# Second attention of a small vision model: queries and keys laid out as four channels of a whole image per partition

## The chip, the cores and the metric

One core of a Trainium2 chip runs the whole program. The metric is device time in microseconds (us) from one launch, the median of several runs.

## What is computed

The model has two layers on 8 images of 16x16 pixels with 192 channels. Each layer adds an attention and then a mixture of experts to its input. The change touches the attention of the second layer only:

```python
def _dilate_attention(q, k, v, head_dim, scale, ksz, dil):
    qr = q.reshape(B, nh, head_dim, L)
    kp = _unfold(k, ksz, dil).reshape(B, nh, head_dim, kk, L)
    vp = _unfold(v, ksz, dil).reshape(B, nh, head_dim, kk, L)
    attn = jnp.einsum('bncl,bnckl->bnlk', qr, kp) * scale
    attn = jax.nn.softmax(attn, axis=-1)
    out = jnp.einsum('bnlk,bnckl->bnlc', attn, vp)
...
for g in range(G):
    qkv = jnp.einsum('oi,bihw->bohw', qkv_w, xg[g])
    qkv = qkv.reshape(nd, 3, B, gd // 3, H, W)
    for i in range(nd):
        outs.append(_dilate_attention(qkv[i, 0], qkv[i, 1], qkv[i, 2], hd, scale, KSZ, DILATIONS[i]))
```

Here a pixel attends to its 3x3 neighbours (kk = 9) at a distance of 1, 2 or 3 pixels (the dilation), zero outside the image. There are 4 groups and 8 images, so 32 group-images for each dilation, and a head of 16 channels.

## The kernel before

The program runs in stages, one after the other on five engines: the first attention, the first mixture of experts (MoE), the second attention (about 455 to 612 us of the profiled span), the second MoE. Each engine executes its own list of instructions in the order in which the code below issues them, and waits on semaphores.

In the second attention the dilations are worked through in the order 3, 2, 1 (index i = 2, 1, 0 in the code; `position(i)` is 0, 1, 2). TensorE makes queries, keys and values (L1865), ScalarE copies them from PSUM to `stage` (L1956), and they are stored to the DRAM tensor `qkvd` in three phases of four DMAs (`store_qkv`: phase 0 on SyncE's queue, phases 1 and 2 on GpSimd's). Then they are loaded back in another layout (`load_qkv`, L1688): the first queries by GpSimd, all the rest by SyncE, in the order keys of dilation 3; queries, keys of dilation 2, values of dilation 3; queries, keys of dilation 1, values of dilations 2 and 1. SyncE waits for the stores of a phase before the loads that need them.

The layout before: a partition holds one group-image and one quarter of the rows (4 quarters x 32 group-images = 128 partitions), with all 16 channels of 4 rows of 16 pixels. Keys (`k1`, in the tile `kk`) and values (`v1`, in `qq`) carry a halo of d rows above and below, whose rows outside the image ScalarE fills with zeros during the first MoE (`clear_edges`, L1696). Queries (`q1`) lie in `pk` and `xn`. VectorE clears the border columns of the products once, before it combines the first MoE's results (`clear_columns`).

The work per dilation, with three groups of three neighbours (a group `col` has one horizontal shift; the first, here called the middle column, has none):

- `products` (VectorE, L1761): nine multiplications of queries by shifted keys into `prod`, one buffer for all dilations, so a group waits until TensorE has read the same group of the dilation before.
- `channel_sums` (TensorE, L1877): for each group 16 matmuls, one per channel, with the 128x128 identity as weights, 3 x 64 columns each, summed in PSUM. A matmul in float32 is two records in the profile.
- `scores` (VectorE), `exponentials` (ScalarE), `weights` (VectorE): the softmax over nine neighbours; ScalarE's `copy_scores` brings the sums from PSUM first.
- `values` (VectorE, L1789): nine products of weights and shifted values into six `term` buffers. For dilation 3 all nine terms go to TensorE; for dilations 2 and 1 VectorE adds two of each three itself (L1819), and TensorE gets six.
- `neighbour_sums` (TensorE, L1895): two matmuls with the identity for each term, one per half of the channels.
- `value_sums` (ScalarE, L1974): the copy of the sum from PSUM, then SyncE stores it to `y1d`.

The order on each engine is written out by hand. VectorE: products(2), products(1), scores(2), products(0, 0), weights(2), values(2), products(0, 1), products(0, 2), scores(1), weights(1), values(1), scores(0), weights(0), values(0). TensorE: channel_sums(2), channel_sums(1), neighbour_sums(2), channel_sums(0), neighbour_sums(1), neighbour_sums(0), then 12 filler matmuls (L1930) while the result goes through DRAM. ScalarE:

```python
copy_scores(2)
exponentials(2)
copy_scores(1)
value_sums(2)
exponentials(1)
copy_scores(0)
exponentials(0)
value_sums(1)
value_sums(0)
```

## Time and profile before

| | us |
|---|---|
| median of 3 runs (lowest to highest) | 837.42 (832.13 to 838.84) |
| the profiled execution | 838.17 |
| its span, first to last instruction | 836.4 |
| TensorE busy in the span | 750.3 (90%) |
| VectorE busy | 412.8 (49%) |
| ScalarE busy | 305.1 (36%) |
| GpSimd busy | 384.2 (46%) |

Times in the trace are us from the start of the span. PE is TensorE (matmuls), PEld its weight loads, DVE VectorE, ACT ScalarE, POOL GpSimd, SP SyncE. L1761 is line 1761 of the kernel. Each row of a group of instructions ends with the time for which the engine had stood idle before them, and with what ended that. TensorE overlaps its matmuls, so the mean duration of one is longer than the time by which it moves the work on; that time is the length of a run of matmuls divided by their number.

### The profile page before, as it was taken

Reading aid. Unit: us, or ns where it says so; the run is one execution under the profiler, and the core shown is the slowest. Engines: PE = TensorE matmul, PEld = TensorE weight load, DVE = VectorE, ACT = ScalarE, POOL = GpSimd, SP = SyncE. Lnnn points to the kernel's source line nnn. Section 1 sums busy time; section 2 is a strip of 40 time slices with the busy share of each in tenths; the row PEclk is TensorE's granted clock in tenths of the full one; section 3 lists DMA queues with packets and bytes.
Section 4 is the critical chain, followed back from the end, with each engine's and each line's share of the span. In section 5 each row is a group of like instructions: output and inputs, shape, how many; then the busy total and the mean of one; then the engine's idle time right before and its main releaser. Section 6 shows DMA issues by size and latency. Waiting matters only on the chain.

```text
span 836.4 us, 19543 instructions
## 1 busy us (share of the span) xinstructions
PE 750.3 (90%) x6156; PEld 642.6 (77%) x6157; DVE 412.8 (49%) x999; ACT 305.1 (36%) x862; POOL 384.2 (46%) x789
## 2 busy tenths in 40 slices
PE   7989999999988999999980689998987999999980
PEld 4768878888745999999980459783655999999980
DVE  4354564567566333433316336998276333433315
ACT  2434464455651423424340640011260433424330
POOL 8754453420134677777731030000044677777730
PEclk9797999999998999999995699999998999999995
DMA  7595663663683111111104199400794111111106
GB/s 239 165 213 139 154 147 105 168 133 75 218 302 128 42 48 53 40 55 55 49 18 150 37 263 196 72 26 25 272 337 138 46 49 53 45 55 51 44 17 226
DMA packets 61082, 97.21 MB, mean 116 GB/s; under 512 B 25711, under 2 KB 43844, under 8 KB 61032
## 3 DMA queue, kind: packets, MB, share of 16 engines
q1 hardware_dynamic: 43560, 62.28, 27.2%
q0 software_dynamic: 17472, 34.27, 13.8%
q8 instruction: 31, 0.51, 0.3%
q14 instruction: 19, 0.16, 0.1%
HBM read 66.23 MB, written 31.52 MB: 117 GB/s over the span
## 4 chain that ended last, share of the span: by engine, by line
PE 58%; DVE 13%; issue 10%; POOL 9%; DMA 5%; ACT 2%; SPq 1%; POOLq 1%; DVEq 0%; ACTq 0%
PE ps L1498 11%; PE ps L1482 9%; PE ps L1490 5%; PE ps L779 4%; PE ps L1877 4%; DVE x_sb L1425 3%; PE ps L809 2%; POOL credit L1554 2%; POOL yd L1572 2%; PE ps L1895 2%; DVE arena L1789 2%; PE ps L829 2%; PE ps L755 2%; POOL xnT L1562 2%; PE ps L853 2%
## 5 line engine op out<-in xcount | busy, mean ns | idle before, releaser
L1536 ACT ACTIVATE arena<-ps,b1s 128x128 f32<-128x128 f32 x468 | 123.9, 410 | 241.4 <-PE ps L1490 241.3
L1498 PE MATMUL ps<-arena 128*128 x936 | 158.7, 329 | 1.2 <-ACT arena L1536 1.2
L1498 PEld LDWEIGHTS ps<-arena 128*128 128x128 f32 x936 | 151.4, 190 | 3.7 <-issue 1.6
L1482 PE MATMUL ps<-xnT 128*128 128x128 f32 x936 | 112.2, 280 | 1.9 <-DVE xnT L1376 1.9
L1482 PEld LDWEIGHTS ps<-xnT 128*128 128x128 f32 x936 | 111.0, 197 | 2.3 <-DVE xnT L1376 2.3
L275 POOL TENSOR_TENSOR rstd<-veps,cst 128x4 f32<-128x4 f32 (+1 forms) x12 | 14.9, 1238 | 191.0 <-DVE veps L269 191.0
L1554 POOL TENSOR_TENSOR credit<-credit 1x1 f32<-1x1 f32 x306 | 70.4, 230 | 48.1 <-DVE xnT L1382 19.0
L1562 POOL DMA_INDIRECT xnT<-xnd,gcur x78 | 79.1, 1014 | 17.4 <-issue 12.4
L626 DVE TENSOR_REDUCE rt<-ps 98x2 f32<-98x392 f32 x96 | 53.0, 563 | 65.8 <-PE ps L809 65.8
L1388 DVE COPY xnT<-arena 128x768 f32 x78 | 43.9, 563 | 69.2 <-PE ps L1482 65.9
L1572 POOL DMA_INDIRECT yd<-rt,scur x52 | 57.7, 1110 | 27.0 <-issue 20.6
L1068 ACT ACTIVATE arena<-ps 98x392 f32<-98x392 f32 x96 | 46.7, 499 | 63.6 <-PE ps L829 63.2
L1490 PE MATMUL ps<-xnT,rt 64*128 64x128 f32 x936 | 59.2, 278 | 0.0
L1382 DVE TENSOR_TENSOR rt<-ps,xn 128x192 f32<-128x192 f32 x52 | 18.6, 358 | 80.5 <-PE ps L1498 80.5
L1490 PEld LDWEIGHTS ps<-xnT,rt 64*128 64x128 f32 x936 | 54.3, 188 | 3.1
L1877 PE MATMUL ps<-arena,cst 128*128 128x192 f32 x288 | 48.9, 334 | 3.3 <-DVE arena L1761 3.3
L1877 PEld LDWEIGHTS ps<-arena,cst 128*128 128x128 f32 x288 | 48.5, 195 | 4.0 <-DVE arena L1761 3.7
L809 PE MATMUL ps<-kk,qq 114*98 114x196 f32 x192 | 43.0, 309 | 1.9 <-DMA kk<-kd 1.6
L779 PEld LDWEIGHTS ps<-xnT,arena 128*112 128x112 f32 (+2 forms) x448 | 37.0, 173 | 7.7 <-issue 3.9
L779 PE MATMUL ps<-xnT,arena 128*112 128x32 f32 (+4 forms) x448 | 39.6, 261 | 3.6 <-POOL xnT L571 3.6
L1394 DVE COPY rt<-arena 128x384 f32 x78 | 28.3, 363 | 28.1 <-PE ps L1490 25.0
L1895 PE MATMUL ps<-arena,cst 128*128 128x512 f32 (+3 forms) x84 | 34.1, 558 | 3.1 <-DVE arena L1819 3.1
(216 smaller groups left out, 1243.5 us busy)
## 6 DMA issues: line engine op xcount, KB each, us to landing
arena<-in_w SPq DMA_DIRECT2D x16, 576.0 KB, 10.3
arena<-in_w1a SPq DMA_DIRECT2D x16, 384.0 KB, 6.7
arena<-yd SPq DMA_DIRECT2D x8, 768.0 KB, 7.1
kk<-kd SPq DMA_DIRECT2D x48, 96.0 KB
qq<-qd SPq DMA_DIRECT2D x16, 264.0 KB
qq<-qd SPq DMA_DIRECT2D x16, 192.0 KB
arena<-in_w1b SPq DMA_DIRECT2D x16, 192.0 KB, 7.0
qkvd<-arena POOLq DMA_DIRECT2D x8, 384.0 KB, 8.2
```

The source lines that it names most:

```text
L626: m = nc.vector.tensor_reduce(mxa[0:WAH, cc, 2 * u:2 * u + 2, j], ps[0:WAH, SM + u, 0:2 * WA].rearrange("p (q n) -> p q n", q=2), AX.X, AL ...
L779: last = mm(o, relt[w][0:rows, at, 0:cols], q, start=True, stop=True)
L809: last = mm(ps[0:WAH, SM + u, c * WA:(c + 1) * WA], q[:, at:at + WAH], k[:, u * WA:(u + 1) * WA], start=True, stop=True)
L1482: last = mm(hidden(r, f), wcura[r][:, f * P:(f + 1) * P], xgT[r][:, 0, :], start=f < 2, stop=False, skip_group_check=True)
L1490: last = mm(hidden(r, f), wcurb[r][rows, f // 2 * P:(f // 2 + 1) * P], xgT[r][rows, 1, :], start=False, stop=f >= FT - 2, skip_group_check ...
L1498: last = mm(product(r), hidT[r][:, f, :], w2s[:, e, f, :], start=f == 0, stop=f == FT - 1)
L1536: last = nc.scalar.activation(hidT[r][:, f, :], hidden(r, f), ACT.Gelu, bias=b1s[l][:, bass.ds(e * FT + f, 1)])
L1554: nc.gpsimd.tensor_tensor(credit[0:1, 12 + kind:13 + kind], credit[0:1, 0:1], credit[0:1, 0:1], ALU.add)\
L1562: nc.gpsimd.indirect_dma_start(out=xg[r], out_offset=None, in_=xnd[l], in_offset=bass.IndirectOffsetOnAxis(ap=gcur[:, r:r + 1], axis=0))\
L1572: nc.gpsimd.indirect_dma_start(out=yd[l], out_offset=bass.IndirectOffsetOnAxis(ap=scur[:, r:r + 1], axis=0), in_=ys[r], in_offset=None, bo ...
L1877: last = mm(to.rearrange("p (n x) -> p n x", n=3), ident, prod[:, 3 * col:3 * col + 3, c, :], start=c == 0, stop=c == HD - 1)
L1895: last = mm(dst, ident, src, start=k == 0, stop=k == len(terms) - 1, skip_group_check=True)
```

## The change

Queries and keys get another layout: a partition now holds one group-image and a quarter of the channels (4 channels, `CHQ`), for the whole image of 256 pixels. No halo is needed for them, since all rows are in the partition. Each load of queries or keys is four DMAs of 32 partitions x 4 channels x 256 pixels, so runs of 1 KB. Products are formed over the part of the image for which the neighbour exists, so rows outside the image are skipped, too; `clear_columns` clears the border rows of `prod` besides its border columns, and the zeros in the key halos (six of ScalarE's twelve instructions) go. The channel sum now runs over 4 channels in a partition and over 4 groups of partitions: for each channel and each quarter of the pixels, one matmul with a 128x32 weight matrix `fold` (four identities of 32 on top of one another, appended to the constants) sums the four partition groups and writes the 32 partitions of that pixel quarter, so that the scores come out in the layout that the softmax and the values had before. There are still 16 matmuls per group of neighbours. Values keep their layout. VectorE's additions of value products go: TensorE sums nine terms for every dilation.

```diff
@@ -146,7 +146,7 @@
         at = 0
         CST, CST_AT = {}, {}
         for name, n in (("ident", 128), ("rev", E), ("lt", E * E), ("tok", TILES), ("iots", SLOTS), ("ones", 1), ("power", 1),
-                        ("tri", P // 2), ("iot", P // 2), ("mask", 2 * TILES * E + E), ("slots", SLOTS // 2)):
+                        ("tri", P // 2), ("iot", P // 2), ("mask", 2 * TILES * E + E), ("slots", SLOTS // 2), ("fold", 32)):
             CST[name], CST_AT[name] = cst[:, at:at + n], at
             at += n
         ident = CST["ident"]
@@ -1631,23 +1631,24 @@
 
             return max(0, -dx * d), SIDE - d * abs(dx)
 
-        k1, v1, k_edges = [], [], []
+        CHQ = HD // 4
+        k1 = [kk[:, i * CHQ * PIX:(i + 1) * CHQ * PIX].rearrange("p (c y x) -> p c y x", c=CHQ, x=SIDE).bitcast(F32)
+              for i in range(len(DIL))]
+        v1, edges = [], []
         at1 = 0
         for d in DIL:
             n = HD * halo(d) * SIDE
-            for views, home in ((k1, kk), (v1, qq)):
-                rows_ = home[:, at1:at1 + n].rearrange("p (c y x) -> p c y x", c=HD, x=SIDE)
-                views.append(rows_.bitcast(F32))
-                k_edges += [rows_[0:32, :, 0:d, :], rows_[96:P, :, QR + d:QR + 2 * d, :]]
+            rows_ = qq[:, at1:at1 + n].rearrange("p (c y x) -> p c y x", c=HD, x=SIDE)
+            v1.append(rows_.bitcast(F32))
+            edges += [rows_[0:32, :, 0:d, :], rows_[96:P, :, QR + d:QR + 2 * d, :]]
             at1 += n
         q_home = [pk[:, :, :].rearrange("p h n -> p (h n)").bitcast(F32)[:, k * HD * QPIX:(k + 1) * HD * QPIX] for k in range(2)]
         q_home.append(xn[:, :, :, :].rearrange("p u t c -> p (u t c)")[:, 0:HD * QPIX])
-        q1 = [home.rearrange("p (c y x) -> p c y x", c=HD, x=SIDE) for home in q_home]
+        q1 = [home.rearrange("p (c y x) -> p c y x", c=CHQ, x=SIDE) for home in q_home]
 
         stage = ar(0, [QKV_UNITS, GRP * PIX], KC)
-        prod = ar(QKV_UNITS * GRP * PIX, [NN, HD, QPIX])
+        prod = ar(QKV_UNITS * GRP * PIX, [NN, CHQ, PIX])
         term = [ar(k * HD * QPIX, [HD, QPIX]) for k in range(TERMS)]
-        second_term = ar(TERMS * HD * QPIX, [HD, QPIX])
         acc = [ar((TERMS + 1 + i) * HD * QPIX, [QPIX * HD]) for i in range(3)]
         yl = xt_(0, [TILES, C])
         sc = [rt[:, i * NN * QPIX:(i + 1) * NN * QPIX] for i in range(3)]
@@ -1678,9 +1679,13 @@
 
             d = DIL[i]
             dst = (q1, k1, v1)[t]
-            src = qkvd[:, (i * 3 + t) * SPU:(i * 3 + t + 1) * SPU].rearrange("c b g x -> (b g) c x")
-            edge = d if t else 0
-            for quarter in range(4):
+            units = slice((i * 3 + t) * SPU, (i * 3 + t + 1) * SPU)
+            src = qkvd[:, units].rearrange("c b g x -> (b g) c x")
+            for quarter in range(4 if t < 2 else 0):
+                eng.dma_start(dst[i][quarter * 32:(quarter + 1) * 32].rearrange("p c y x -> p c (y x)"),
+                              src[:, quarter * CHQ:(quarter + 1) * CHQ]).then_inc(s_(f"{'qkv'[t]}_in{i}"), 16)
+            edge = d
+            for quarter in range(4 if t == 2 else 0):
                 lo = max(0, quarter * QR - edge)
                 hi = min(SIDE, (quarter + 1) * QR + edge)
                 row = lo - (quarter * QR - edge)
@@ -1691,7 +1696,7 @@
         def clear_edges(act):
 
             zero = CST["lt"][:, 0:1]
-            for edge in k_edges:
+            for edge in edges:
                 parts = edge.shape[0]
                 nc.scalar.activation(edge, zero[0:parts].unsqueeze(2).unsqueeze(3).broadcast_to(list(edge.shape)), ACT.Copy)\
                     .then_inc(s_("edges_clear"), 1)
@@ -1700,13 +1705,17 @@
 
             rows_ = prod.rearrange("p n c (y x) -> p n (c y) x", x=SIDE)
             d = max(DIL)
+            nc.vector.memset(prod[:, 0:NN:3, :, 0:d * SIDE], 0.0)
+            nc.vector.memset(prod[:, 2:NN:3, :, (SIDE - d) * SIDE:PIX], 0.0).then_inc(s_("rows_clear"), 1)
+            v.wait_ge(s_("rows_clear"), 1)
             nc.vector.memset(rows_[:, 3:6, :, 0:d], 0.0)
-            nc.vector.memset(rows_[:, 6:9, :, SIDE - d:SIDE], 0.0)
+            nc.vector.memset(rows_[:, 6:9, :, SIDE - d:SIDE], 0.0).then_inc(s_("columns_clear"), 1)
+            v.wait_ge(s_("columns_clear"), 1)
 
         def attn1_sync(sp):
 
             store_qkv(sp, 0)
-            sp.wait_ge(s_("edges_clear"), len(k_edges))
+            sp.wait_ge(s_("edges_clear"), len(edges))
             sp.wait_ge(s_("qkv_out0"), 16 * STORES)
             load_qkv(sp, 2, 1)
             sp.wait_ge(s_("qkv_out1"), 16 * STORES)
@@ -1729,7 +1738,7 @@
         def attn1_pool(pool):
             for b in range(BLKS):
                 ln_power(pool, 2, range(b, b + 1))
-            pool.wait_ge(s_("edges_clear"), len(k_edges))
+            pool.wait_ge(s_("edges_clear"), len(edges))
             pool.wait_ge(s_("qkv_out0"), 16 * STORES)
             load_qkv(pool, 2, 0)
             store_qkv(pool, 1)
@@ -1756,9 +1765,13 @@
                     v.wait_ge(s_(f"k_in{i}"), 4 * 16)
                 if pos:
                     v.wait_ge(s_("qk_sum"), 3 * (pos - 1) + col + 1)
-                x0, w = columns(DIL[i], NEIGH[3 * col][1])
+                d = DIL[i]
                 for n in range(3 * col, 3 * col + 3):
-                    last = vec.tensor_tensor(in_columns(prod[:, n], i, n), q1[i][:, :, :, x0:x0 + w], shifted(k1, i, n), ALU.mult)
+                    dy, dx = NEIGH[n]
+                    (y0, h), (x0, w) = columns(d, dy), columns(d, dx)
+                    last = vec.tensor_tensor(prod[:, n].rearrange("p c (y x) -> p c y x", x=SIDE)[:, :, y0:y0 + h, x0:x0 + w],
+                                             q1[i][:, :, y0:y0 + h, x0:x0 + w],
+                                             k1[i][:, :, y0 + dy * d:y0 + dy * d + h, x0 + dx * d:x0 + dx * d + w], ALU.mult)
                 last.then_inc(s_("qk_prod"), 1)
 
             def by_neighbour(s):
@@ -1789,7 +1802,7 @@
                 return vec.tensor_tensor(in_columns(to, i, n), shifted(v1, i, n),
                                          weight.unsqueeze(1).broadcast_to([P, HD, QR, w]), ALU.mult)
 
-            made, pairs = [0], [0]
+            made = [0]
 
             def next_term():
 
@@ -1804,20 +1817,8 @@
                 if position(i) == 0:
                     for phase in range(3):
                         v.wait_ge(s_(f"qkv_out{phase}"), 16 * STORES)
-                    for n in range(NN):
-                        value_product(i, n, next_term()).then_inc(s_("pv_term"), 1)
-                    return
-                for col in range(3):
-                    value_product(i, 3 * col + 2, next_term()).then_inc(s_("pv_term"), 1)
-                    a_ = next_term()
-                    if pairs[0]:
-                        v.wait_ge(s_("pv_term"), made[0] - 2)
-                    value_product(i, 3 * col, a_)
-                    value_product(i, 3 * col + 1, second_term).then_inc(s_("pair"), 1)
-                    pairs[0] += 1
-                    v.wait_ge(s_("pair"), pairs[0])
-                    vec.tensor_tensor(in_columns(a_, i, 3 * col), in_columns(a_, i, 3 * col), in_columns(second_term, i, 3 * col),
-                                      ALU.add).then_inc(s_("pv_term"), 1)
+                for n in range(NN):
+                    value_product(i, n, next_term()).then_inc(s_("pv_term"), 1)
 
             for i in (2, 1):
                 for col in range(3):
@@ -1834,6 +1835,7 @@
             scores(0)
             weights(0)
             values(0)
+            v.wait_ge(s_("pv_term"), NN * len(DIL))
             for u in range(2):
                 vec.memset(rt[KC:KC + 1, u * 2 * BT:u * 2 * BT + BT], 1.0).then_inc(s_("y_ones"), 1)
 
@@ -1873,26 +1875,27 @@
                 for col in range(3):
                     pe.wait_ge(s_("qk_prod"), 3 * pos + col + 1)
                     to = ps[:, SCORES[pos][col // 2], col % 2 * 3 * QPIX:(col % 2 + 1) * 3 * QPIX]
-                    for c in range(HD):
-                        last = mm(to.rearrange("p (n x) -> p n x", n=3), ident, prod[:, 3 * col:3 * col + 3, c, :],
-                                  start=c == 0, stop=c == HD - 1)
+                    for c in range(CHQ):
+                        for q in range(4):
+                            last = mm(to[q * 32:(q + 1) * 32].rearrange("p (n x) -> p n x", n=3), CST["fold"],
+                                      prod[:, 3 * col:3 * col + 3, c, q * QPIX:(q + 1) * QPIX],
+                                      start=c == 0, stop=c == CHQ - 1, skip_group_check=True)
                     last.then_inc(s_("qk_sum"), 1)
 
             made = [0]
 
             def neighbour_sums(i):
                 pos = position(i)
-                terms = [n // 3 for n in range(NN)] if pos == 0 else [n // 2 for n in range(6)]
-                for k, col in enumerate(terms):
+                for n in range(NN):
                     m = made[0]
                     made[0] += 1
                     pe.wait_ge(s_("pv_term"), m + 1)
-                    x0, w = columns(DIL[i], NEIGH[3 * col][1])
+                    x0, w = columns(DIL[i], NEIGH[n][1])
                     for half in range(2):
                         cs = slice(half * HD // 2, (half + 1) * HD // 2)
                         src = term[m % TERMS][:, cs].rearrange("p c (y x) -> p (c y) x", x=SIDE)[:, :, x0:x0 + w]
                         dst = ps[:, SUMS[pos] + half, :].rearrange("p (r x) -> p r x", x=SIDE)[:, :, x0:x0 + w]
-                        last = mm(dst, ident, src, start=k == 0, stop=k == len(terms) - 1, skip_group_check=True)
+                        last = mm(dst, ident, src, start=n == 0, stop=n == NN - 1, skip_group_check=True)
                     last.then_inc(s_("pv_sum"), 1)
 
             channel_sums(2)
@@ -1969,7 +1972,7 @@
 
             def value_sums(i):
                 pos = position(i)
-                act.wait_ge(s_("pv_sum"), (9, 15, 21)[pos])
+                act.wait_ge(s_("pv_sum"), NN * (pos + 1))
                 u = SUMS[pos]
                 nc.scalar.activation(acc[i].rearrange("p (x c) -> p c x", c=HD),
                                      ps[:, u:u + 2, :].rearrange("p u (c x) -> p (u c) x", x=QPIX), ACT.Copy)\
@@ -2218,7 +2221,8 @@
         np.eye(P, dtype=f), np.tile((E - e).astype(f), (P, 1)), np.tile((e[None, :] < e[:, None]).astype(f).reshape(-1), (P, 1)),
         (token + 1).astype(f), np.tile(s.astype(f), (P, 1)), halfwords(np.ones((P, 2))),
         np.full((P, 1), -0.5, f), halfwords(p[:, None] < p[None, :]),
-        halfwords(np.tile(p, (P, 1))), halfwords(np.concatenate(list(sums), 1)), halfwords(np.tile(s, (P, 1)))], 1)
+        halfwords(np.tile(p, (P, 1))), halfwords(np.concatenate(list(sums), 1)), halfwords(np.tile(s, (P, 1))),
+        np.tile(np.eye(32, dtype=f), (P // 32, 1))], 1)
     return {k: np.ascontiguousarray(o[k]) for k in INPUTS}
```

On TensorE, from the last matmul of the queries, keys and values (L1865) to the fillers (L1930, in the new code L1933), the rows of the channel sums (L1877, now L1880) and of the value sums (L1895, now L1898) differ as follows.

```order
-L1865 MATMUL ps<-xnT,wqkv 96x256 x48
-L1877 MATMUL ps<-arena,cst 128x192 x96
-L1895 MATMUL ps<-arena,cst 128x512 x6
-L1895 MATMUL ps<-arena,cst 128x32x13 x12
-L1877 MATMUL ps<-arena,cst 128x192 x48
-L1895 MATMUL ps<-arena,cst 128x512 x4
-L1895 MATMUL ps<-arena,cst 128x32x14 x8
-L1895 MATMUL ps<-arena,cst 128x512 x4
-L1895 MATMUL ps<-arena,cst 128x32x15 x8
-L1930 MATMUL ps<-cst 128x512 x12
```

In the changed kernel the same place on TensorE reads:

```order
+L1867 MATMUL ps<-xnT,wqkv 96x256 x48
+L1880 MATMUL ps<-arena,cst 32x192 x96
+L1898 MATMUL ps<-arena,cst 128x512 x6
+L1898 MATMUL ps<-arena,cst 128x32x13 x12
+L1880 MATMUL ps<-arena,cst 32x192 x48
+L1898 MATMUL ps<-arena,cst 128x512 x6
+L1898 MATMUL ps<-arena,cst 128x32x14 x12
+L1898 MATMUL ps<-arena,cst 128x512 x6
+L1898 MATMUL ps<-arena,cst 128x32x15 x12
+L1933 MATMUL ps<-cst 128x512 x12
```

The order stays; the 144 channel-sum matmuls write 32 rows instead of 128, and the value sums of dilations 2 and 1 grow from 12 matmuls to 18 each.

On VectorE, the values of dilation 2 and the first row after them stood so before (L1819 is the addition, L1770 the next maximum):

```order
L1789 TENSOR_TENSOR arena<-qq,rt 128x1024 x3
L1819 TENSOR_TENSOR arena<-arena 128x1024
L1789 TENSOR_TENSOR arena<-qq,rt 128x64x14 x3
L1819 TENSOR_TENSOR arena<-arena 128x64x14
L1789 TENSOR_TENSOR arena<-qq,rt 128x64x14 x3
L1819 TENSOR_TENSOR arena<-arena 128x64x14
L1770 TENSOR_REDUCE rt<-rt 128x64
```

They are now nine products with nothing between them. The products of dilation 3 (L1772), which were three of 1024 elements and six of 832, now read:

```order
+L1772 TENSOR_TENSOR arena<-xn,kk 128x4x208
+L1772 TENSOR_TENSOR arena<-xn,kk 128x1024
+L1772 TENSOR_TENSOR arena<-xn,kk 128x4x208
+L1772 TENSOR_TENSOR arena<-xn,kk 128x4x13x13
+L1772 TENSOR_TENSOR arena<-xn,kk 128x64x13
+L1772 TENSOR_TENSOR arena<-xn,kk 128x4x13x13 x2
+L1772 TENSOR_TENSOR arena<-xn,kk 128x64x13
+L1772 TENSOR_TENSOR arena<-xn,kk 128x4x13x13
```

Their number and place are the same; six of the nine are over fewer elements than before.

## Rows read from the trace of the kernel before

**Rows 1.** Chain that ended last, in order of time: start us, us, what

```profile
487.96 7.42 DMA xn<-qkvd
...
498.95 33.15 PE ps L1877 x192
532.10 13.65 PE ps L1895 x36
545.77 1.95 ACT arena L1974
...
584.57 10.30 PE ps L1930 x24
```

**Rows 2.** Timeline of VectorE: start us, us, engine, line, operation, out<-in, count, idle before

```profile
495.40 9.11 DVE L1761 TENSOR_TENSOR arena<-xn,kk 128x1024 f32<-128x1024 f32 x9 [28.20 <-DMA xn<-qkvd]
512.15 9.51 DVE L1761 TENSOR_TENSOR arena<-pk,kk 128x1024 f32<-128x1024 f32 x9 [7.64 <-DMA kk<-qkvd]
521.57 1.14 DVE L1770 TENSOR_REDUCE rt<-rt 128x64 f32<-128x576 f32 x1
522.75 0.76 DVE L1772 TENSOR_TENSOR rt<-rt 128x576 f32<-128x576 f32 x1
...
527.66 1.14 DVE L1778 TENSOR_REDUCE rt<-rt 128x64 f32<-128x576 f32 x1
...
530.21 9.11 DVE L1789 TENSOR_TENSOR arena<-qq,rt 128x1024 f32<-128x1024 f32 x9
```

**Rows 3.** VectorE's groups by line, 494 to 584 us: busy us, mean ns, idle before

```profile
L1789 DVE TENSOR_TENSOR arena<-qq,rt 128x1024 f32<-128x1024 f32 x9 | 10.5, 1220 | 0.1
L1789 DVE TENSOR_TENSOR arena<-qq,rt 128x960 f32<-128x960 f32 x6 | 6.6, 1152 | 0.0
L1761 DVE TENSOR_TENSOR arena<-xn,kk 128x832 f32<-128x832 f32 x6 | 5.7, 1018 | 0.0
L1819 DVE TENSOR_TENSOR arena<-arena 128x1024 f32<-128x1024 f32 (+2 forms) x6 | 7.0, 1158 | 0.2
```

**Rows 4.** TensorE: a value product (L853, timeline and line view), and L1877

```profile
77.47 1.52 PE L853 MATMUL ps<-arena 98*17 98x196 f32 x32
L853 PEld LDWEIGHTS ps<-arena x384: 92/98/98, 77.5 to 230.0; 98*17 98x17 f32 x192
545.57 15.76 PE L1877 MATMUL ps<-arena,cst 128*128 128x192 f32 x96
```

**Rows 5.** DMA of 512 to 528 us, of 446 to 450, and L1688

```profile
DMA packets 8266, 3.06 MB, mean 191 GB/s; under 512 B 6617, under 2 KB 8265, under 8 KB 8265
DMA packets 1008, 1.50 MB, mean 375 GB/s; under 512 B 32, under 2 KB 1008, under 8 KB 1008
DMA to landing us min/median/max: 3.1/5.7/8.6
```

**Rows 6.** Timeline of DMA issues on SyncE's and GpSimd's queues, before the second products

```profile
485.33 1.97 SPq L1688 DMA_DIRECT2D kk<-qkvd  x4
488.60 2.06 POOL L1674 DMA_DIRECT2D qkvd<-arena  x4
499.26 2.76 SPq L1688 DMA_DIRECT2D pk<-qkvd  x4
```

**Rows 7.** Windows: us, busy us of each engine, granted clock (PEclk), DMA share, GB/s

```profile
455.00:472.00 17.00, 6.95 (x30) 5.42 (x31) 11.10 (x49) 10.86 (x34) 2.95 (x3) 0.50 0.00 0
499.00:512.00 13.00, 13.00 (x70) 13.00 (x71) 5.51 (x6) 0.49 (x1) 0.00 (x0) 0.87 1.20 249
```

**Rows 8.** Clearings (timeline, line view), and the waits that stand beside them

```profile
437.41 0.54 DVE L1703 MEMSET arena<- 128x576 f32 x1
445.67 1.41 DVE L1425 SCALAR_TENSOR_TENSOR x_sb<-arena,gw,x_sb 128x192 f32<-128x192 f32 x4 [7.12 <-DMA arena<-yd]
L1696 ACT ACTIVATE kk<-cst x6: 399/627/842, 245.1 to 250.3; 32x256 fp32r<-32x256 f32 x2, 32x512 fp32r<-32x512 f32 x2, 32x768 fp32r<-32x768 f32 x2
257.89 0.19 POOL L1559 COPY gcur<-gidx 128x1 int32<-128x1 int32 x1 [11.76 <-DVE gidx L1350]
```

## Prediction, made before the changed kernel ran

> **What bounds the kernel now.** I read the chain that ended last first, then VectorE's timeline through the second attention, then the groups by line and shape, then the DMA windows. The chain [rows 1] enters the second attention through the landing of the first queries (DMA, until 495.4 us), then lies on TensorE without a break from 498.95 to 545.75: 33.15 us of channel sums for dilations 3 and 2, then 13.65 us of value sums for dilation 3. After ScalarE's copy it goes to VectorE and ends with the last value sum at 584.57. VectorE's timeline [rows 2] shows a second chain beside it: the products of dilation 2 start only at 512.15, after 7.64 us idle, because their keys landed then; from there VectorE is hardly idle. So there are three limits close together: loads, channel sums, VectorE work. Relaxing one alone gives little; the change touches all three.
>
> **VectorE work.** One operation takes, by the busy sums, 10.5/9 = 1.167 us for 1024 elements, 6.6/6 = 1.10 for 960 and 5.7/6 = 0.95 for 832 [rows 3]; that is near 1.05 ns an element plus a little, and 896 comes to 1.02. Products over a whole image drop rows outside the image too: a side column of dilation 3 has 4x13x13 = 676 elements for the shifted rows, which no row shows. By the slope that is 0.79 us; if it cost as much as the nearest row, 0.95. I take 0.79, since 832 elements in runs of 13 are on the same slope as whole runs; likewise 0.90 (784) and 1.02 (900). Dilation 3: 2x0.95+1.167, then twice 2x0.79+0.95, 8.1 us against 9.11 [rows 2]. Dilation 2: 8.8 against 9.51. Dilation 1: 3.3 for the middle column and 6.3 for the sides, against 10.0. The six additions of value products go: 7.0 us [rows 3], in exchange for six more terms on TensorE. A value sum takes 13.65 us for 36 matmul records [rows 1], which is 12 of 512 and 24 of 416 columns, 0.846 ns a column; so nine terms take 14.3 us for dilation 2 and 14.9 for dilation 1.
>
> **Channel sums.** Now 96 records take 15.76 us, 0.164 us each [rows 4]. Each record becomes a 32-column one, and four in turn write four partition groups. The first attention's value products do the same with 17 columns and 196 moving ones: 32 records in 1.52 us [rows 4], 0.048 us each, where one alone costs 0.164. I take 1.52 us a column of neighbours, against 5.25 now. Bounds: 0.041 us (a quarter of 0.164) and, if nothing overlaps and each weight load of 0.098 us [rows 4] shows, 0.262.
>
> **Loads.** Queries and keys of one dilation go from 4096 packets of 256 to 640 bytes to 1024 packets of 1 KB. Where such small ones fill the engines, 8266 packets pass in 16 us at 191 GB/s; packets of 1536 bytes pass at 375 [rows 5]. No row has 1 KB packets: 1.05 MB takes 2.8 us at the one rate and 5.5 at the other. I take 2.8, the nearer in kind (not packet-bound). For the first queries, issued by GpSimd with the last starting at 487.96 [rows 1], landing took 7.42 us among 4096 packets; the shortest landing on this line is 3.1 [rows 5]. So VectorE starts between 491.1 and 495.4; I take 491.5. SyncE issued the next loads at 499.26, when the stores that GpSimd issued from 488.60 to 490.66 had landed [rows 6]. With 3072 packets fewer before them I take 494.5 (last issue plus the shortest landing, 493.8, and a margin). Eight issues at 0.5 us (1.97 for four [rows 6]) and a landing of 3.1 put the keys of dilation 2 at 501.5. Bounds: 499.6, where the products of dilation 3 end, and 512.15 as now. The values of dilation 3 and the loads of dilation 1 follow by 508 to 512, just before their use.
>
> **The new chain.** 491.5 + 8.1 = 499.6, wait to 501.5, dilation 2 to 510.3. TensorE, one column behind, is done at 511.9. Scores (a reduction and a subtraction, 1.95 us [rows 2]) to 512.3, middle column of dilation 1 to 515.6, weights (530.21 - 527.66 = 2.56 [rows 2]) to 518.2, first value product at 519.4. TensorE has then stood for over 7 us. After its wait before 498.95 its mean clock over 499 to 512 was 0.87, and in the short bursts of 455 to 472 it was 0.50 [rows 7], the lower of its two levels (1.2 of 2.4 GHz); what the wait before 498.95 cost is the shortfall, 0.13 x 13 = 1.7 us, and I take the same here. Value sum of dilation 3: 519.4 + 13.6 + 1.7 = 534.7. This is a new wait: ScalarE's queue holds the copy of that sum (1.95 us [rows 1]) ahead of the exponentials of dilation 2, so these end at 537.5 although VectorE, after values (9.1 us), side columns (6.3) and scores, was ready at 535.6; VectorE stands 1.9 us, and behind it everything. Weights to 540.1, values 9.6 to 549.7, scores, exponentials (0.75 with the wait) and weights to 555.0, first product at 556.1. TensorE did the channel sums of dilation 1 by 539.3 and the second value sum by 555.6, so it is free, and the last value sum ends at 556.1 + 14.9 = 571.0. That is 13.6 us before 584.57.
>
> Costs hidden: two more row clearings like that of 0.54 us [rows 8] and their waits lie before the DMA that VectorE waits for until 445.67 (7.12 us idle [rows 8]); uncovered they would cost 1.3. Six of the edge clearings, 0.6 us each, go from ScalarE [rows 8], but GpSimd waits there for VectorE until 257.89 [rows 8], so I count 0 (at most 3.8 gained). The constants grow by 16 KB: 0.1 us at most. After 584.57 nothing changes: the same stores, filler matmuls and loads follow the last copy.
>
> Sum: 838.17 - 13.6 = 824.6 on the profiled execution, which is 0.75 above the median shown; so 823.9.
>
> On the clock: the Trainium skill, "TensorE: Matmul & The Clock Gate", section "A second HAM failure mode: psum-queue depth-cycling", says that a TensorE which idles briefly between groups of matmuls swings between its two levels and pays at each return. Rows of this case agree for bursts ([rows 7], 0.50) and not for the dense 499 to 512. By that rule the time is that of the second rival; by the row alone it is the 1.7 us already counted.
>
> **Rivals.**
> First, the loads come no sooner (stores, not packets, hold them). For: the stores are 3.1 MB and unchanged, and go on at the same time. Against: the small-packet rate [rows 5]. Products of dilation 2 start at 512.15 as now, 10.65 us later than in my chain; the end is 581.7, the gain 2.9, the time 834.5 on the median.
> Second, TensorE falls to its lower level in the short waits. For: 0.50 in bursts [rows 7]. Against: the value sums are dense once begun. Channel sums of dilation 1 then take 9.1 us instead of 4.6, so the second value sum starts at 543.9; with 1.7 us more in it and in the last, the end is 543.9 + 14.3 + 1.7 + 14.9 + 1.7 = 576.5, the time 829.4.
> Third, slower than before: the four groups follow one another and show their weight loads. TensorE is then the chain from 495.7 on: 288 records of r us and three value sums, 495.7 + 288 r + 42.9. At r = 0.112 this passes my end, at 0.160 it equals the present one, at 0.164 the time is 838.7, and with 0.098 us of load on top, 866.9; from r = 0.189 it is over 1% slower. For: the 32-column weights are wider than 17, and every matmul reloads them. Against: 0.048 us in [rows 4].
>
> **How the numbers follow.** My forecast has 0.70, the loads rival 0.12, the clock rival 0.10, the serial rival 0.06, and 0.02 is something slower that I don't see. A measurement of this kernel tells about 1% from no change, which is 829.0 on the fast side. The forecast's own range is 819.5 to 829: 819.5 is loads at 499.6 (-1.9), no clock loss (-1.2) and the low bounds of products and overlap (-1.3); 829 is loads some 5 us later than taken. The full range runs from 819 to 834.5, which takes in the first two rivals. Faster by over 1%: 0.70 and half of the clock rival, 0.75. Within 1%: 0.12, the other half and a sixth of the serial rival, 0.18. Slower: 0.07.
>
> **What would show it.** Right: a column of channel sums spans about 1.5 us at full clock; VectorE's first wait ends near 491.5 and the products of dilation 2 start by 502; the SyncE issues after the first stores start near 494.5; no addition between value products; three value sums of about 14 to 15 us; the wait of VectorE for the exponentials of dilation 2. Wrong: the products of dilation 2 waiting for keys past 506; channel sums above 3.6 us a column; a clock of 0.50 inside the value sums beyond their start; an end of the last value sum later than 576.

## The result, and the profile after

The changed kernel takes 832.5 us (median of 12 runs, 825.43 to 836.85) against 838.9 us for the kernel before beside it (12 runs, 832.13 to 845.04): ratio 0.9921, 95% interval 0.9893 to 0.995. It is faster by 6.4 us, where 13.5 were forecast (837.42 - 823.9); the time lies inside the range given, nearer to its upper end.

The profiled execution has a span of 831.3 us. The stages ahead of the change differ by up to 13 us from one execution to the next, in kernels that have the same code there. So every mark is counted from S, the start of SyncE's first store in the second attention (476.69 us before, 478.77 after). The clearings and the edge zeros, which the prediction counted as hidden, lie ahead of S; S lies at 470.43 to 483.48 in the profiles of the changed kernel and its variants, and at 476.69 and 480.25 in the two profiles with the code before (one of them is r5, below), so no cost or gain of theirs can be told from that spread. What follows the stage takes the same time in both: 252.0 us before (836.4 - 584.40), 251.8 after (831.3 - 579.50).

The chain that ended last, after (start us, us, what), to be read beside [rows 1]:

```profile
491.93 7.06 DMA qkvd<-arena
502.88 4.25 DMA pk<-qkvd
507.12 2.36 issue
527.12 16.45 PE ps L1898 x36
548.65 9.51 DVE arena L1802 x9
564.58 15.08 PE ps L1898 x36
579.66 10.30 PE ps L1933 x24
```

The 33 us of channel sums are off the chain. In their place stands a DMA chain: a store that lands at 499, then the loads of dilation 2. VectorE's timeline (the number in brackets is the idle time before a row), beside [rows 2]:

```profile
493.97 8.06 DVE L1772 TENSOR_TENSOR arena<-xn,kk 128x832 f32<-128x832 f32 x9 [24.58 <-DMA xn<-qkvd]
509.49 8.77 DVE L1772 TENSOR_TENSOR arena<-pk,kk 128x896 f32<-128x896 f32 x9 [7.46 <-issue]
520.05 3.35 DVE L1772 TENSOR_TENSOR arena<-pk,kk 128x960 f32<-128x960 f32 x3
533.40 1.03 DVE L1802 TENSOR_TENSOR arena<-qq,rt 128x832 f32<-128x832 f32 x1 [0.32 <-PE ps L1898]
535.12 1.03 DVE L1802 TENSOR_TENSOR arena<-qq,rt 128x832 f32<-128x832 f32 x1 [0.69 <-PE ps L1898]
546.03 1.21 DVE L1791 TENSOR_REDUCE rt<-rt 128x64 f32<-128x576 f32 x1 [1.88 <-ACT rt L1971]
```

VectorE still idles 7.46 us before the products of dilation 2 (7.64 before). The row names no releaser ("issue"); VectorE waits there for queries and keys, and SyncE's issues of the keys (below) end at 506.17, 3.3 us before it starts. TensorE's timeline, beside [rows 4]:

```profile
497.70 1.51 PE L1880 MATMUL ps<-arena,cst 128*32 128x192 f32 x32
512.77 7.17 PE L1880 MATMUL ps<-arena,cst 128*32 128x192 f32 x96 [9.18 <-DVE arena L1772]
527.12 16.44 PE L1898 MATMUL ps<-arena,cst 128*128 128x512 f32 x36 [7.18 <-DVE arena L1802]
543.49 4.11 PE L1880 MATMUL ps<-arena,cst 128*32 128x192 f32 x96
549.93 14.44 PE L1898 MATMUL ps<-arena,cst 128*128 128x512 f32 x36 [2.33 <-DVE arena L1802]
564.58 15.08 PE L1898 MATMUL ps<-arena,cst 128*128 128x512 f32 x36 [0.21 <-DVE arena L1802]
```

A column of channel sums takes 1.51 us, and three in a row 4.11. The value sum of dilation 3 takes 16.44. SyncE's issues, beside [rows 6], and the DMA traffic of 499 to 503 us by queue (q0: GpSimd's stores, q1: SyncE's loads; packets, MB, share of the 16 engines' time), then of 503 to 509.5:

```profile
499.00 4.32 SPq L1685 DMA_DIRECT2D pk<-qkvd  x4
503.36 2.81 SPq L1685 DMA_DIRECT2D kk<-qkvd  x4
```

```profile
q0 software_dynamic: 263, 0.92, 84.4%
q1 hardware_dynamic: 98, 0.09, 6.6%
...
DMA packets 1916, 1.54 MB, mean 237 GB/s; under 512 B 656, under 2 KB 1877, under 8 KB 1915
```

Counted from S, SyncE issues the first of these loads 2.3 us sooner than before (S + 20.2; before S + 22.6, 499.26 in [rows 6]). The eight issues take 7.2 us, and for four microseconds almost only stores move. Windows of the first channel sums of dilation 2 and of the first value sum (us, busy times, granted clock, DMA share, GB/s), beside [rows 7]:

```profile
510.00:515.00 5.00, 2.23 (x28) 1.38 (x32) 5.00 (x6) 0.00 (x0) 0.00 (x0) 0.50 1.19 211
...
525.00:530.00 5.00, 2.88 (x4) 1.33 (x5) 4.93 (x6) 0.00 (x0) 0.00 (x0) 0.50 0.30 44
530.00:535.00 5.00, 5.00 (x11) 2.08 (x10) 4.11 (x5) 0.00 (x0) 0.00 (x0) 0.77 0.00 0
```

### The profile page after: what moved, and what is told of

Read it like the earlier page. It is cut to its first block, busy times and chain, and to the rows that moved or that the text cites. A ratio compares the mean times of both kernels' runs of the same rounds, so it can differ in the third digit from the quotient of the medians.

```text
span 831.3 us, 19577 instructions
## 1 busy us (share of the span) xinstructions
PE 729.8 (88%) x6180; PEld 609.5 (73%) x6181; DVE 405.6 (49%) x995; ACT 301.1 (36%) x856; POOL 381.1 (46%) x789
## 3 DMA queue, kind: packets, MB, share of 16 engines
q0 software_dynamic: 17472, 34.27, 14.3%
## 4 chain that ended last, share of the span: by engine, by line
PE 42%; POOL 17%; issue 16%; DVE 13%; DMA 7%; ACT 2%; POOLq 1%; SPq 1%; DVEq 0%; ACTq 0%
PE ps L1498 5%; POOL credit L1554 5%; PE ps L1482 5%; POOL xnT L1562 4%; PE ps L1898 4%; PE ps L779 3%; POOL yd L1572 3%; DVE x_sb L1425 3%; PE ps L1490 2%; PE ps L809 2%; PE ps L829 2%; PE ps L755 2%; DMA kk<-kd 2%; PE ps L853 2%; DVE arena L1802 1%
## 5 line engine op out<-in xcount | busy, mean ns | idle before, releaser
L275 POOL TENSOR_TENSOR rstd<-veps,cst 128x4 f32<-128x4 f32 (+1 forms) x12 | 14.9, 1238 | 184.3 <-DVE veps L269 184.2
L1554 POOL TENSOR_TENSOR credit<-credit 1x1 f32<-1x1 f32 x306 | 68.6, 224 | 48.5 <-DVE xnT L1382 19.2
L1490 PE MATMUL ps<-xnT,rt 64*128 64x128 f32 x936 | 59.2, 278 | 0.0
L1898 PE MATMUL ps<-arena,cst 128*128 128x512 f32 (+3 forms) x108 | 46.0, 586 | 9.7 <-DVE arena L1802 9.7
L1898 PEld LDWEIGHTS ps<-arena,cst 128*128 128x128 f32 x108 | 21.1, 198 | 33.8 <-issue 21.7
L1394 DVE COPY rt<-arena 128x384 f32 x78 | 28.1, 360 | 30.9 <-PE ps L1490 26.4
L809 PEld LDWEIGHTS ps<-kk,qq 114*98 114x98 f32 x192 | 26.6, 174 | 15.2 <-issue 11.9
```

Source lines behind the costliest of these rows:

```text
L809: last = mm(ps[0:WAH, SM + u, c * WA:(c + 1) * WA], q[:, at:at + WAH], k[:, u * WA:(u + 1) * WA], start=True, stop=True)
L1490: last = mm(hidden(r, f), wcurb[r][rows, f // 2 * P:(f // 2 + 1) * P], xgT[r][rows, 1, :], start=False, stop=f >= FT - 2, skip_group_check ...
L1554: nc.gpsimd.tensor_tensor(credit[0:1, 12 + kind:13 + kind], credit[0:1, 0:1], credit[0:1, 0:1], ALU.add)\
L1898: last = mm(dst, ident, src, start=n == 0, stop=n == NN - 1, skip_group_check=True)
```

## The experiments

Marks of all profiles in us after S: start of the products of dilation 3 and of dilation 2, start of the middle-column products of dilation 1 ("middle"), end of the last value sum (start of the idle matmuls behind it). "Predicted" is the prediction's own chain, less 476.69; its end follows the mark of the chain ([rows 1]: 584.57; 579.66 after), which lies 0.2 us behind the start of the idle matmuls. Each kernel has one profile. With the same loads a mark still varies: the start of dilation 2 lies between 30.4 and 31.7 in the six kernels with the changed kernel's loads (changed, r4, r6, r11, r13, r14), and between 24.7 and 26.2 in the three with r9's (r9, r12, r15). A difference of 1.5 us in one mark shows little by itself.

| kernel | dil. 3 | dil. 2 | middle | end | middle to end |
|---|---|---|---|---|---|
| before | 18.7 | 35.5 | 47.6 | 107.7 | 60.2 |
| predicted | 14.8 | 24.8 | 35.6 | 94.3 | 58.7 |
| changed | 15.2 | 30.7 | 41.3 | 100.7 | 59.4 |
| one DMA (r1) | 15.0 | 31.8 | 42.8 | 101.6 | 58.8 |
| two DMAs (r2) | 15.8 | 30.8 | 41.4 | 100.9 | 59.5 |
| stores after (r3) | 14.9 | 26.7 | 43.0 | 101.8 | 58.8 |
| additions back (r4) | 15.0 | 30.8 | 41.4 | 103.5 | 62.1 |
| terms alone, on before (r5) | 18.8 | 35.3 | 47.1 | 113.5 | 66.4 |
| clock held (r6) | 15.2 | 30.5 | 41.0 | 99.5 | 58.4 |
| keys first, four (r7) | 15.2 | 27.2 | 47.2 | 108.2 | 60.9 |
| keys first, one (r8) | 14.9 | 24.9 | 44.9 | 104.1 | 59.2 |
| order of need, one (r9) | 14.8 | 25.0 | 36.3 | 95.0 | 58.8 |
| order of need, four (r10) | 15.1 | 26.6 | 38.6 | 98.2 | 59.6 |
| clock held, 5 more (r11) | 15.1 | 30.9 | 41.6 | 99.9 | 58.4 |
| combined, 5 (r12) | 14.9 | 24.7 | 36.0 | 94.8 | 58.9 |
| clock held, 2 more (r13) | 15.3 | 30.4 | 40.9 | 98.2 | 57.3 |
| exponentials first (r14) | 15.2 | 31.7 | 42.3 | 100.0 | 57.8 |
| combined, 2 (r15) | 14.8 | 26.2 | 36.8 | 94.1 | 57.2 |

**The loads, first attempt.** One or two transfers for each of the queries and keys instead of four (partition and channel group exchanged, the constant to suit):

```diff
-            for quarter in range(4 if t < 2 else 0):
-                eng.dma_start(dst[i][quarter * 32:(quarter + 1) * 32].rearrange("p c y x -> p c (y x)"),
-                              src[:, quarter * CHQ:(quarter + 1) * CHQ]).then_inc(s_(f"{'qkv'[t]}_in{i}"), 16)
+            pp, ss = P // 1, 32 // 1
+            for part in range(1 if t < 2 else 0):
+                eng.dma_start(dst[i][part * pp:(part + 1) * pp].rearrange("p c y x -> p c (y x)"),
+                              src[part * ss:(part + 1) * ss]).then_inc(s_(f"{'qkv'[t]}_in{i}"), 16)
...
```

> Changed kernel, but a load of queries or keys is one DMA over all 128 partitions instead of four of 32 (the channel quarter becomes the fast part of the partition index, the fold matrix follows). Bytes and 1 KB packets are the same. Times are counted from the first store issue on SyncE (478.77 in the changed kernel's profile); there the products of dilation 3 start at 15.2, those of dilation 2 at 30.7, and the last value sum ends at 100.9. Theory A (a DMA to 32 partitions moves at about half the rate of one to 128, 190 to 240 against 375 GB/s, whatever its packets): the loads of dilation 2 need about 3 us instead of 6.5, so the second products start at 26 to 27.5 and the end is at 96 to 98. Theory B (the stores of the last phase, issued just before, hold the loads up until they are through): the second products start at 29 or later and the end is within 1 us of 100.9. Theory C (the fixed work per 1 KB packet sets the rate): 30 to 31, unchanged but for some 0.5 us of fewer issues.

> As the run with one DMA, but two DMAs of 64 adjacent partitions each. If the rate goes by the part of the memory's ports that a DMA's partitions reach, and 64 adjacent partitions reach no more than 32 do: like four DMAs, second products at 29.5 to 31. If it goes by the number of partitions: halfway, 28 to 29. If the number of issues decides: near the run with one DMA.

Measured: 833.17 us with one (ratio 0.9899, 0.985 to 0.9948; the profile is of the longest of its ten runs, 836.66), 833.87 in a single run with two. The products of dilation 2 start no sooner. With the stores in the way, the shape of the loads decides nothing that these marks can show. Then the stores themselves, moved behind the loads:

```diff
-            for i, t in ((1, 0), (1, 1), (2, 2)):
+            for i, t in ((1, 0), (1, 1)):
                 load_qkv(sp, i, t)
+            store_qkv(sp, 2)
+            load_qkv(sp, 2, 2)
...
-            store_qkv(pool, 2)
```

> Changed kernel, but the four stores of the last phase are issued by SyncE behind the loads of queries and keys of dilation 2, no longer by GpSimd before them. Theory B (stores hold the loads): the loads flow from their issue at about 20.2 on, the second products start at 26 to 27, and the end is at 96 to 98, if the values of dilation 3, now behind the stores, still land by 46. Theory A alone (half rate): the loads still need 5 to 6.5 us after their issue, so 27 to 28. Theory C: as A. No change (30.7) would speak against both.

A single run, 836.02 us. The products of dilation 2 do start 4.0 us sooner, so the stores held their loads; but the end is 101.8 and not the expected 96 to 98: the gain is lost to a new wait for the keys of dilation 1, as VectorE's timeline shows:

```profile
507.76 8.78 DVE L1773 TENSOR_TENSOR arena<-pk,kk 128x896 f32<-128x896 f32 x9 [3.73 <-issue]
...
524.04 3.36 DVE L1773 TENSOR_TENSOR arena<-pk,kk 128x960 f32<-128x960 f32 x3 [5.59 <-DMA kk<-qkvd]
```

**Keys ahead of values, values on the other queue.** Queries and keys of dilation 1 directly behind the last stores on SyncE; the values of dilations 3 and 2 on GpSimd's queue, from the moment when the keys of dilation 2 are there. With four transfers (r7), and with one (r8):

```diff
-            for i, t in ((1, 0), (1, 1), (2, 2)):
+            for i, t in ((1, 0), (1, 1)):
                 load_qkv(sp, i, t)
+            store_qkv(sp, 2)
             sp.wait_ge(s_("qkv_out2"), 16 * STORES)
-            for i, t in ((0, 0), (0, 1), (1, 2), (0, 2)):
+            for i, t in ((0, 0), (0, 1), (0, 2)):
                 load_qkv(sp, i, t)
...
-            store_qkv(pool, 2)
+            pool.wait_ge(s_("k_in1"), 4 * 16)
+            for i in (2, 1):
+                load_qkv(pool, i, 2)
```

> The changed kernel with another order of transfers: the stores of the last phase go from GpSimd's queue to SyncE's, behind the queries and keys of dilation 2; the queries and keys of dilation 1 follow them on SyncE ahead of all values; the values of dilations 3 and 2 go to GpSimd's queue and wait there until the keys of dilation 2 have landed. Still four transfers of 32 partitions for each tensor. Theory A (what was missing is only the order: stores ahead of loads, values ahead of keys): products of dilation 2 start at S + 26.7 as in the run with the stores moved, products of dilation 1 at S + 37.5 to 40 without a wait over 2.5 us, the last value sum ends at S + 97 to 99.5. Theory B (transfers to 32 partitions are slow by themselves): the keys of dilation 1 come at S + 40 to 43 and the end stays near S + 100 to 101. If the values of dilation 3 are late instead, VectorE waits before its first value product, and the end is later by that wait.

> The same order of transfers as the run before it, with each of the queries and keys as one transfer to 128 partitions (partition and channel group exchanged, the constant of the group sums to suit). Theory A (only the order matters): as the run with four transfers, within 1 us at each mark. Theory B (four transfers of 32 partitions are slower by themselves, in their issues and in what they move in a microsecond): products of dilation 2 start at S + 24 (23 to 25), the keys of dilation 1 wait for nothing, and the last value sum ends at S + 96 to 97.5, at least 1.5 us sooner than with four.

839.06 us (ratio 0.9996, 0.997 to 1.0023) and 835.83 (0.9963, 0.9928 to 0.9998): both miss. VectorE waits over 9 us for the keys of dilation 1, in r7:

```profile
502.99 8.78 DVE L1775 TENSOR_TENSOR arena<-pk,kk 128x896 f32<-128x896 f32 x9 [3.99 <-issue]
...
523.02 3.36 DVE L1775 TENSOR_TENSOR arena<-pk,kk 128x960 f32<-128x960 f32 x3 [9.39 <-DMA kk<-qkvd]
```

In r8 the queries and keys of dilation 1 are issued from 500.49 and have landed at 515.32, 14.8 us later, beside the values on the other queue. A second queue did not spare the keys the wait; it put the values beside them. Theory A as written (order alone) fell, because the order across two queues is not an order. One transfer instead of four was worth 2.3 us at the products of dilation 2.

**All later transfers in the order of need, on one queue.** The stores of the middle phase and the first queries stay with GpSimd; the transfers that SyncE issues behind the first keys follow the order of need, the last stores among them. With one transfer (r9) and with four (r10), against the changed kernel:

```diff
-            for i, t in ((1, 0), (1, 1), (2, 2)):
+            for i, t in ((1, 0), (1, 1)):
                 load_qkv(sp, i, t)
+            store_qkv(sp, 2)
             sp.wait_ge(s_("qkv_out2"), 16 * STORES)
-            for i, t in ((0, 0), (0, 1), (1, 2), (0, 2)):
+            for i, t in ((0, 0), (0, 1), (2, 2), (1, 2), (0, 2)):
                 load_qkv(sp, i, t)
...
-            store_qkv(pool, 2)
```

> The changed kernel with all transfers after the first keys on SyncE's queue in the order in which they are needed: queries and keys of dilation 2, the stores of the last phase (taken from GpSimd's queue), queries and keys of dilation 1, then the values of dilations 3, 2 and 1; each of the queries and keys is one transfer to 128 partitions. Nothing of small packets runs beside the stores or the keys any more. Theory (what the loads of the keys waited for are other transfers ahead of them or beside them: 1.57 MB of stores, and the values with their small packets): products of dilation 2 start at S + 25, the stores of the last phase have landed by S + 31, the middle-column products of dilation 1 start at S + 35.6 to 37.5, the values of dilation 3 are there by S + 42, and the last value sum ends at S + 95 to 97.5 against S + 100.7 in the changed kernel. Rival (the transfers have no more to give whatever their order, about 200 GB/s for loads into this layout): the keys of dilation 1 land at S + 40 or later and the end is S + 100 or later.

> The same order of transfers with four transfers of 32 partitions for each of the queries and keys. If four cost about 2.3 us more than one at each place, as between the two runs with the values on GpSimd's queue (27.2 against 24.9 for the products of dilation 2): products of dilation 2 at S + 27, the middle-column products of dilation 1 at S + 38 to 41, the last value sum ends at S + 97.5 to 100. If one or four makes no difference with this order: the marks of the run before it, within 1 us.

r9 takes 825.75 us, ratio 0.9844 (0.9774 to 0.9914, four runs); r10 830.58 in a single run. The marks of r9 are where the theory put them, the values of dilation 3 about 0.4 us late. From the first issue of queries and keys of dilation 1 to their use it takes 6.5 us in r9 (505.80 to 512.25), where r8 took 14.8. VectorE in r9, and the traffic while the keys of dilation 2 load: r9 from 498 to 500 us, then r10 from 499.5 to 502.5 (issued from 498.16):

```profile
500.98 8.78 DVE L1773 TENSOR_TENSOR arena<-pk,kk 128x896 f32<-128x896 f32 x9 [2.10 <-issue]
...
512.25 3.36 DVE L1773 TENSOR_TENSOR arena<-pk,kk 128x960 f32<-128x960 f32 x3 [0.62 <-DMA kk<-qkvd]
...
518.47 9.16 DVE L1803 TENSOR_TENSOR arena<-qq,rt 128x1024 f32<-128x1024 f32 x9 [0.45 <-DMA qq<-qkvd]
```

```profile
DMA packets 662, 0.71 MB, mean 354 GB/s; under 512 B 27, under 2 KB 643, under 8 KB 662
q1 hardware_dynamic: 662, 0.71, 105.4%
```

```profile
DMA packets 774, 0.72 MB, mean 240 GB/s; under 512 B 87, under 2 KB 773, under 8 KB 773
q1 hardware_dynamic: 773, 0.70, 97.4%
```

So the same kilobyte packets pass at 354 GB/s in one transfer to 128 partitions and at 240 in four to 32 each. The four also take longer to issue (4.9 us for the eight of dilation 2 in r10, 1.3 for two in r9). In r10's window packets took 97.4% of the engines' time, so engines idle between issues are not what holds the rate at 240 there; why the packets take longer these runs don't show. The Trainium skill, "SBUF — State Buffer", section "Door 1: The DMA port swizzle", says that the partitions a transfer spans decide how many ports it reaches, and gives 189 GB/s for 32 partitions and 328 for 128 at 1 MiB. The two rows agree with it in that the narrow transfers are slower (240 against 354); they are no test of its figures, since r10 has four transfers of 128 KB in flight, to different partitions.

**Parts of the change by themselves.** The additions put back into the changed kernel (r4), and the nine terms alone put into the kernel before (r5); the edit of r5, of which r4 is the reverse:

```diff
-                    for n in range(NN):
-                        value_product(i, n, next_term()).then_inc(s_("pv_term"), 1)
-                    return
-                for col in range(3):
...
+                for n in range(NN):
+                    value_product(i, n, next_term()).then_inc(s_("pv_term"), 1)
...
-                terms = [n // 3 for n in range(NN)] if pos == 0 else [n // 2 for n in range(6)]
+                terms = [n // 3 for n in range(NN)]
...
```

> Changed kernel, but VectorE adds two of each three value products of dilations 2 and 1 again (six additions back, six terms on TensorE instead of nine). By the prediction's terms the value stage of dilation 2 on VectorE grows by 3.4 us and the last one ends 0.5 us earlier after its weights: the end is 2.9 us later than in the changed kernel, at about 103.8 from the first store issue. If TensorE were the bound here, removing its terms would make it earlier by up to 8 us instead.

> The kernel before with one part of the change alone: nine value terms for each of the three dilations on TensorE and no additions on VectorE; queries, keys, channel sums and loads as before. Times from the first store that SyncE issues in this stage (S). Theory (three limits close together; with the old channel sums TensorE is the bound behind the first value sum): the channel sums of dilation 1 still take 15.8 us behind the value sum of dilation 3, so the value sum of dilation 2 starts no sooner (S + 84.5) and takes 14.4, the last one 15: the last value sum ends at S + 113.5 to 114 against S + 107.7 before, 5.7 to 6.3 us later, ratio to before about 1.007. Rival (VectorE is the bound there and the seven microseconds of additions are simply saved): the end at S + 100.7, ratio 0.992.

r4: 834.28 us (ratio 0.9931, 0.9892 to 0.9971), the end 2.7 us later; by time it can't be told from the changed kernel (0.9921). r5: 848.38 us, ratio 1.0092 (1.005 to 1.0133), the end 5.8 us later than before. By the marks the same edit loses in one kernel and gains in the other, since TensorE is the bound in the one and VectorE in the other. TensorE in r5 has no pause, and VectorE waits for it; in r4 TensorE waits for VectorE (last row):

```profile
549.18 15.76 PE L1866 MATMUL ps<-arena,cst 128*128 128x192 f32 x96
564.77 29.14 PE L1884 MATMUL ps<-arena,cst 128*128 128x512 f32 x72
```

```profile
566.69 1.09 DVE L1789 TENSOR_TENSOR arena<-qq,rt 128x896 f32<-128x896 f32 x1 [5.80 <-PE ps L1884]
```

```profile
566.80 11.42 PE L1912 MATMUL ps<-arena,cst 128*128 128x512 f32 x20 [4.59 <-DVE arena L1803]
```

**The clock and the exponentials.** Idle matmuls in TensorE's pauses (0 in the third place in r6, 5 in r11, 2 in r13), and ScalarE's exponentials ahead of the copy (r14), each on the changed kernel:

```diff
+            def fill(n, bank=3):
+                for _ in range(n):
+                    mm(ps[:, bank, :], ident, cst[:, 0:BT], start=True, stop=True)
+
             channel_sums(2)
+            fill(8)
             channel_sums(1)
+            fill(8)
             neighbour_sums(2)
             channel_sums(0)
+            fill(2, 7)
             neighbour_sums(1)
```

```diff
             copy_scores(1)
-            value_sums(2)
             exponentials(1)
+            value_sums(2)
```

> The changed kernel with eight idle matmuls of 512 columns on TensorE after the channel sums of dilation 3 and eight after those of dilation 2, so that it has less idle time before the first value sum; nothing else is changed. Theory (the clock loss in the first value sum is on the path): the three channel sums of dilation 2 run at full clock, the value sum of dilation 3 takes 13.7 to 14.2 us instead of 16.4, VectorE's two waits for a free term (1.0 us) go and its wait for the exponentials of dilation 2 falls from 1.88 to 0.75 us; the last value sum ends at S + 98.6 (98 to 99) instead of S + 100.7. Rival (the clock loss is hidden by VectorE's own work, or the idle matmuls only delay the real ones): the end stays at S + 100.7 or comes later.

> The changed kernel with the sixteen idle matmuls of the earlier run and five more after the channel sums of dilation 1, in the pause before the value sum of dilation 2, where the clock fell in the earlier run (granted 0.66 from 550 to 555 us). Theory (the clock loss of the first value sum had only moved to the second): both value sums run at full clock, 13.9 and 14.4 us, and the last value sum ends at S + 98.4 to 98.9, the 2.1 us that VectorE had gained. Rival (the second value sum was late for another reason, or the five matmuls delay it): S + 99.5 or later.

> The changed kernel with eight and eight idle matmuls as before and two instead of five after the channel sums of dilation 1: an idle matmul took 0.91 us (two records of 0.456), so five took 4.56 us and held the value sum of dilation 2 back by 1.8 us (551.72 against a first term at 549.9); two take 1.8 us, less than the 2.5 us that TensorE waits there. Theory (the clock loss of the value sum of dilation 3 lies on the path with 2.1 us, and both earlier runs hid that, one by a fall of the clock in the next value sum, one by idle matmuls that were too many): from the start of the middle-column products of dilation 1 to the end of the last value sum 57.3 us (57.1 to 57.6) against 59.45 in the changed kernel, 58.45 and 58.35 in the two runs. Rival (that loss is hidden by VectorE's own work): 58.3 us or more.

> The changed kernel with one thing moved: on ScalarE the exponentials of dilation 2 stand ahead of the copy of the first value sum. Theory (the copy ahead of them in ScalarE's queue is what VectorE waits for): VectorE's wait for these exponentials falls from 1.88 to 0.75 us, and from the start of the middle-column products of dilation 1 to the end of the last value sum the stage is 1.1 us shorter, 58.3 instead of 59.45. Rival (the wait is for the value sum itself or is made up later): 59.4.

r6: 833.37 us (ratio 0.9948, 0.992 to 0.9976), r11 833.25 (0.9962, 0.9926 to 0.9997), r13 832.51 (0.9916, 0.9889 to 0.9943), r14 830.97 in a single run. None can be told from the changed kernel by its time. From the middle column on, r1, r2 and r3, which have the changed kernel's code there, take 58.8 to 59.5 us; r13 (57.3) and r14 (57.8) lie below that, r6 and r11 (58.4) hardly. In r6 the first value sum takes 13.90 us, but the clock falls in the second, and the end is 99.5 and not the expected 98 to 99 (window of r6):

```profile
550.00:555.00 5.00, 5.00 (x9) 2.10 (x8) 5.00 (x6) 0.00 (x0) 0.00 (x0) 0.66 0.00 0
```

In r11 the clock holds at 1.00 throughout, and the five idle matmuls last 4.56 us, which pushes the second value sum behind its first term: the rival of that run, with the end at 99.9. In r13 two fit, and the stage from the middle column on takes 57.3 us, 2.2 less than in the changed kernel, as expected. TensorE in r13:

```profile
527.02 13.90 PE L1898 MATMUL ps<-arena,cst 128*128 128x512 f32 x36 [0.29 <-DVE arena L1802]
540.85 4.11 PE L1880 MATMUL ps<-arena,cst 128*32 128x192 f32 x96
544.88 1.98 PE L1903 MATMUL ps<-cst 128*128 128x512 f32 x4
547.61 14.44 PE L1898 MATMUL ps<-arena,cst 128*128 128x512 f32 x36 [0.74 <-DVE arena L1802]
```

In r14 the wait for the exponentials falls to 0.75 us (VectorE's row), and the stage from the middle column on to 57.8; 1.1 of the 1.7 is that wait, the rest a first value sum of 15.88 us instead of 16.44:

```profile
542.81 1.21 DVE L1791 TENSOR_REDUCE rt<-rt 128x64 f32<-128x576 f32 x1 [0.75 <-ACT rt L1971]
```

**Together.** r9 with idle matmuls (8 after dilation 2, then 5 in r12, 2 in r15) and the exponentials first:

> The changed kernel with the transfers in the order of need, one transfer for each of the queries and keys, idle matmuls after the channel sums of dilation 2 (eight) and of dilation 1 (five), and ScalarE's exponentials of dilation 2 ahead of its copy of the first value sum. By the sum of the parts: the end of the run with the order of need, less 2.1 us for the clock and the wait for the exponentials: S + 93 to 95.5, 5 to 7.5 us sooner than the changed kernel, ratio to before 0.983 to 0.988. If the parts hide one another (the idle matmuls delay the value sums, or VectorE waits for the values instead), the end is that of the run with the order of need alone or later.

> The combined kernel with two idle matmuls instead of five after the channel sums of dilation 1. In the combined run the transfers in the order of need put the middle-column products of dilation 1 at S + 36.0, and the end at S + 94.8, 58.9 us later, because the five idle matmuls held the value sum of dilation 2 until 542.2 where its first term was there at 540.4. Theory: 57.3 us (plus up to 0.6 for the wait for the values of dilation 3) after the middle-column products, the last value sum ends at S + 93 to 93.9, ratio to before 0.981 to 0.986. Rival (no more to gain there): S + 94.8, as the combined run.

r12: 825.89 us, ratio 0.9846 (0.979 to 0.9903), its end no sooner than r9's for the reason of r11. r15: 827.71 us, ratio 0.9849 (0.9801 to 0.9897); its middle-to-end is the expected 57.2 us, but its middle came 0.6 us later than in r9, so the end is 1.0 sooner only. All three beat the kernel before. Their medians lie 4.8 to 6.8 us below the changed kernel's and their ends 5.7 us or more, though their intervals overlap its own (0.9893 to 0.995) a little. By time they can't be told from one another.

## Why the prediction was half right

**VectorE work: right.** Nine products of dilation 3 took 8.06 us (8.1 predicted) and of dilation 2 8.77 (8.8). The additions' removal is worth 2.7 us on the path in the changed kernel (r4), and value sums of nine terms took 14.44 and 15.08 us (14.3, 14.9).

**Channel sums: right.** 1.51 us a column (1.52). The third rival, four groups one after the other with their weight loads, is out. (Its 495.7 has no working; 491.5 and three products of 3.07 us give 494.6.)

**Loads: the step that failed.** The start of VectorE was right (S + 15.2 against 14.8, from 491.5). The keys of dilation 2 were taken for 501.5, S + 24.8, and came at S + 30.7, 5.9 us later. That sum has three terms (they make 501.6), and two of them failed:

- SyncE's first issue was put at 494.5, S + 17.8, and came at S + 20.2, 2.4 us later. The stores that it waits for were given 3.1 us behind their last issue, the shortest landing on the line of the loads (L1688, [rows 5]), and a margin. The last of them took 7.06 us from the start of its issue (491.93), and in the kernel before 8.6 us had passed behind these issues (490.66 to 499.26 in [rows 6]).
- The eight issues were put at 4 us and took 7.2 (499.00 to 506.17). The 0.5 us each came from four issues in 1.97 us; [rows 6] has 2.76 for the queries of dilation 2 themselves.
- The landing behind the last issue was put at 3.1 us and is 3.3 (506.17 to 509.49).

Behind the second term and a part of the first stands one assumption: that the last stores, on the other queue, cost nothing. In the first four microseconds the loads moved 0.09 MB beside 0.92 of the stores; with the stores behind them (r10) the same loads, issued from 498.16, moved 0.70 MB between 499.5 and 502.5, their issues took 4.9 us, and the first came at S + 19.3, 0.9 us sooner. The runs part the 5.9 us: 4.1 go when the stores stand behind the loads (30.7 to 26.6, r10), 1.6 more with one transfer to 128 partitions (25.0, r9), which is about what a mark varies, but r7 and r8 show it too (2.3), and the 0.2 left is within what marks vary. The rate of 375 GB/s is no term of that sum; it fits the one transfer (354) and not the four of the changed kernel (240).

That is the first rival's mechanism (the stores hold the loads) at about half its price (5.9 us later than the chain, of 10.65): it was held to mean no gain at all in this wait, and given 0.12. The smaller number of packets probably matters too (the first queries landed in 4.1 us, 7.4 before), but no run here takes it alone. A case in which both count was not among those of the prediction.

**The new chain: its form right, one size off.** From the middle column on, the prediction has 58.7 us, the trace 59.4 (59.6 to the mark of the chain, which the prediction used). The wait for the exponentials was put at 1.9 us and is 1.88; r14 shows that ScalarE's order makes it. The clock's loss in the value sum of dilation 3 was put at 1.7 us and is 2.8 beside the 13.6 of the prediction (16.44), or 2.5 beside the 13.90 of r13. Two pauses stand before it (9.18 and 7.18 us), and the channel sums between them already ran at 0.50. But the pauses don't explain its size: without idle matmuls this sum takes from 15.29 (r9) to 16.80 us (r7), and 15.70 in r3 behind a pause of 13.03; what sets it is not shown.

In r9 the end came at S + 95.0 against the predicted 94.3, at a measured ratio of 0.9844 where 823.9 of 837.42 is 0.984. So the rest of the chain holds once the loads come in order, but that r9 meets the forecast so closely is in part luck. Its first issue comes at S + 18.8, 1.0 us later than forecast, its two issues take 1.3 us instead of 4, and the products start 4.9 us behind them instead of 3.1; its loss of 1.7 us in the first value sum is the smallest of the kernels without idle matmuls.

**The second rival** (lower clock level in short waits) was partly so: the channel sums of dilation 2 ran at 0.50, but the value sums of dilations 2 and 1 at 1.00 in the changed kernel. With the rule of the Trainium skill that the prediction weighed ("TensorE: Matmul & The Clock Gate", section "A second HAM failure mode: psum-queue depth-cycling") the trace agrees in those channel sums and not in the two value sums. The clock's whole price on the path is small: r13 takes both clock and wait away and gains 2.2 us in the stage (1.5 beside r1 and r3).

**In numbers:** the chain was to end 13.6 us sooner in the stage and ends 7.0 us sooner (107.7 - 100.7; the measured time fell by 6.4). The 6.6 us between are 5.9 from the loads, less 0.2 between the products of dilation 2 and the middle column (10.6 us for 10.8), plus 0.9 behind it (59.6 for 58.7).

## What to carry to other kernels

When a change shrinks the work behind a load, price the load by all that is in flight beside it, on every queue: what the store it waits for takes to land, how long its own issues take, and which bytes share the engines. Put transfers into one queue in the order in which they are needed before counting a sooner start, and don't expect a second queue to keep two of them apart. An edit's worth belongs to the engine that is the bound when it is made: the nine terms cost 5.8 us by themselves and gained 2.7 after the channel sums had become short.

## What was not expected of the hardware

Two queues did not share by need: in 499 to 503 us of the changed kernel GpSimd's stores moved 0.92 MB in 263 packets beside 0.09 MB in 98 packets of loads that had been issued from 499.00 on. Holding TensorE's clock in one pause moved its fall to a later pause (granted 0.66 in r6 at 550 to 555 us, after 2.64 us without work), where the changed kernel with a pause of 2.33 us had stayed at 1.00; why these two differ is not shown.
